# A graph network on one core: edge counts are made during both attention passes, their sort comes first, the maximum sweeps run beside the sage products

## The chip, the cores and the metric

The kernel is written in Bass for Trainium2 and runs on one core of one chip. Its engines (PE for products, DVE for vector work, ACT for activations, POOL, SP for DMA) each run their own list of instructions in order, and wait for each other by semaphores. The metric is the device time of one execution in microseconds, lower is better. Before the change the median of three runs is 3654.17 us (3653.41 to 3660.13).

## The reference, cut to what matters

3125 nodes with 128 features and 50000 edges, sorted by target. Four graph layers follow each other, each with a residual and a layer norm:

```python
x = layernorm(x + L0(x))   # edge MLP on [x[src], edge_attr], mean over each target's edges, node MLP
x = layernorm(x + L1(x))   # two attention convolutions ("gat1" 4 heads, "gat2" 1 head)
x = layernorm(x + L2(x))   # three sage convolutions: h @ Ws + (segment_sum(h[src], dst) / deg) @ Wn + b
x = layernorm(x + L3(x))   # softmax aggregation: m = x[src] + edge_attr, segment_max, exp, segment_sum
```

L2 needs, for every pair of nodes, how many edges go from one to the other; the kernel makes these counts itself and then sums neighbours by matrix products. L3's segment_max is split: the maximum of the edge features over each target's run is found by running scans over the edges, forwards and backwards, which need no node value.

## The kernel before, in words

Nodes are 26 tiles of 128 (NT). Edges are 391 blocks of 128 (NB); in the edge passes they are 416 steps (S), four to a group, 104 groups (NG).

**Order of stages.** Head: loads, tables, a sort of the edges into steps. "mlp" pass over the 104 groups (edge_products, add_node_terms, exponentials_of_hidden, join_hidden, sum_hidden, add_sums). Node work. gat1 pass, node work, gat2 pass (attention_pass on each engine). Sort of the steps of counting (place_windows on PE, sort_into_windows and place_steps on DVE). Layer norm. Counting (count_edges on PE, mark_cells on DVE, read_pairs on ACT, store_counts on SP). Sage (sum_neighbours on PE, convert on ACT and DVE, load_counts on SP). Layer norm. Pool pass. Output.

**An edge pass.** POOL gathers the rows of four steps for each group by indirect DMA (L712 for mlp, L725 for gat, L739 for pool). In mlp the ring takes 12 groups; in gat 24. The pass loops on every engine are written out by slot q. In a gat slot DVE does: the batch stages of eight groups (logits, carries, maxima; L1768 to L1817), add_sums of group q - 13 (L1561), weigh of group q - 11 (L1838, L1840, which read the turned weights in PSUM), mark_nodes of q + 1 (L1741, from a row that SP loads, L584, two buffers), and one sweep (L1759 in gat1, L1761 in gat2). PE sums the weighted rows (L955) after weigh.

**Sweeps.** 196 scans of 128 x 512 (SWEEPS = 2 x 98). SP loads 256 KB of values and 128 KB of borders for each (L599, L601) and stores 256 KB (L609), two buffers each way. Sweep v waits for the store of sweep v - 2.

**Counting.** The sorted edges are cut into 598 steps (BUILD), each at most 128 edges of one window of 16 targets (SPAN; 208 windows). A step is two products into a bank of PSUM: a product with zeros that clears it if its window is new (L1036), and low_marks x cell_marks (L1039). DVE makes these two bf16 marks of each step by is_equal (L2103, L2105). Two steps make a pair; ACT copies both banks to 16-bit counts (L1367), SP stores two rows of 100 KB (L649). Two chains run, one from each end, on two banks each, and are joined where they meet (MEET = 300).

**Sage.** The counts are loaded by chunks of 512 targets (L661, WIDTHS = six of 512 and one of 128, per layer, three layers). ACT converts the even and DVE the odd of 25 slices of a chunk to float (L1377, L2126), seven slices in hand (SLICES); PE multiplies each (L1116), in sage1 twice. The load of chunk n waits until chunk n - 2 is converted. PE makes the own part of the chunk before after slice 10 (L1053 to L1062) and its rows after slice 20 (L1084 to L1090).

## Time and profile before

| | us |
|---|---|
| median of three runs | 3654.17 |
| profiled execution, device time | 3656.58 |
| its span, first to last instruction | 3654.7 |

The page cuts the span into 40 slices of 91 us. Digits are tenths of the slice that each engine is busy; PEclk is TensorE's granted clock, DMA the share of the 16 DMA engines.

```profile
## 2 busy tenths in 40 slices
PE   6777778344444423444453777789999995666666
PEld 4665665234444323344342333335544543555554
DVE  5888885567777756787667666621111226666668
ACT  2887886334433232433322666633211234444443
POOL 4777760477777357777730000000000004777770
PEclk9999999655555555555556999989999997888886
DMA  6555550577777266777710545453321334555550
GB/s 205 154 160 155 161 143 11 140 194 201 205 198 203 51 169 176 201 196 206 198 36 14 163 162 164 161 157 92 98 72 45 108 117 112 148 148 151 150 147 26
```

POOL's line shows the four gathering passes (slices 1 to 6, 8 to 14, 15 to 21, 34 to 39). Between slices 21 and 33 POOL has nothing to do: sort and norm, counting (DMA at 5), then sage (PE at 9).

### The profile page before, as it was taken

The numbers are of one execution on the slowest core, as the hardware profiler recorded it, in microseconds if no ns is written. First come the engines' busy times: TensorE is split into PE (matmuls) and PEld (weight loads), VectorE is DVE, ScalarE is ACT, GpSimd is POOL, SyncE is SP. The second block draws the span as 40 slices with busy tenths as digits, with TensorE's granted clock in tenths as the row PEclk, the third lists the DMA queues.
The fourth block names the chain that finished last, engine by engine and source line by source line (L and its number), as shares of the span: only waits on it lengthen the run. The fifth ranks groups of instructions, "written<-read, shape, count | busy, mean of one in ns | idle before, by whom it ended". The sixth has DMA issues, their size and how long they took to land.

```text
span 3654.7 us, 44760 instructions
## 1 busy us (share of the span) xinstructions
PE 2391.6 (65%) x9865; PEld 1648.7 (45%) x9865; DVE 2257.3 (62%) x6047; ACT 1621.9 (44%) x3304; POOL 1622.4 (44%) x1620
## 2 busy tenths in 40 slices
PE   6777778344444423444453777789999995666666
PEld 4665665234444323344342333335544543555554
DVE  5888885567777756787667666621111226666668
ACT  2887886334433232433322666633211234444443
POOL 4777760477777357777730000000000004777770
PEclk9999999655555555555556999989999997888886
DMA  6555550577777266777710545453321334555550
GB/s 205 154 160 155 161 143 11 140 194 201 205 198 203 51 169 176 201 196 206 198 36 14 163 162 164 161 157 92 98 72 45 108 117 112 148 148 151 150 147 26
DMA packets 675621, 511.58 MB, mean 140 GB/s; under 512 B 66405, under 2 KB 641758, under 8 KB 675024
## 3 DMA queue, kind: packets, MB, share of 16 engines
q1 hardware_dynamic: 614422, 370.87, 34.6%
q0 software_dynamic: 57904, 132.57, 14.5%
q10 hardware_dynamic: 3052, 5.38, 0.5%
q8 instruction: 94, 1.54, 0.2%
q14 instruction: 149, 1.22, 0.1%
HBM read 385.39 MB, written 123.19 MB: 139 GB/s over the span
## 4 chain that ended last, share of the span: by engine, by line
PE 28%; POOL 27%; DVE 16%; issue 14%; SPq 8%; DMA 3%; DVEq 2%; ACT 1%; POOLq 0%; ACTq 0%
POOL big L725 16%; PE ps L1116 15%; POOL y_and_h L739 11%; SPq L649 6%; PE ps L856 5%; DVE y_and_h L1589 3%; DVE big L1561 3%; DVE ps L1581 2%; PE ps L792 1%; SPq L644 1%; DMA big<-table_gat,big 1%; PE ps L778 1%; DVEq L494 1%; PE ps L955 1%; DVE w_sb L1759 1%
## 5 line engine op out<-in xcount | busy, mean ns | idle before, releaser
L725 POOL DMA_INDIRECT big<-table_gat,big x832 | 854.3, 1027 | 480.8 <-issue 247.8
L739 POOL DMA_INDIRECT y_and_h<-table_pool,src_block x391 | 396.5, 1014 | 1309.6 <-DMA table_pool<-x_sb 1190.7
L1561 DVE TENSOR_TENSOR big<-big,ps 128x257 f32 (+3 forms) x1664 | 590.8, 355 | 226.3 <-issue 22.4
L955 PE MATMUL ps<-y_and_h,work 128*128 128x136 f32 (+1 forms) x1664 | 437.0, 443 | 413.1 <-DVE y_and_h L1840 393.1
L955 PEld LDWEIGHTS ps<-y_and_h,work 128*128 128x128 f32 x1664 | 373.6, 325 | 443.1 <-DVE y_and_h L1840 442.9
L712 POOL DMA_INDIRECT big<-table_mlp,src_block x391 | 370.9, 948 | 158.8 <-issue 117.6
L1304 ACT ACTIVATE work<-iota,dst_rel 128x128 f32<-128x128 f32 x936 | 296.0, 387 | 68.8 <-PE ps L955 68.8
L1326 ACT ACTIVATE y_and_h<-y_and_h 128x128 f32<-128x128 f32 (+1 forms) x26 | 8.0, 309 | 670.9 <-DVE y_and_h L1817 670.9
L1367 ACT ACTIVATE work<-ps 128x800 uint16<-128x800 f32 x298 | 244.5, 836 | 136.3 <-DMA adjacency<-work 84.3
L856 PE MATMUL ps<-w_sb,work 128*128 128x256 f32 x832 | 210.9, 398 | 127.7 <-DVE y_and_h L1589 116.9
L1147 PE MATMUL ps<-big,y_and_h 128*128 x624 | 203.1, 483 | 129.5 <-DVE big L2210 128.3
L1036 PE MATMUL ps<-work 128*128 128x400 bf16 x598 | 211.3, 353 | 100.7 <-ACT work L1367 91.3
L856 PEld LDWEIGHTS ps<-w_sb,work 128*128 128x128 f32 x832 | 152.4, 193 | 185.7 <-DVE y_and_h L1589 158.0
L2103 DVE TENSOR_SCALAR work<-work,big 128x128 bf16<-128x128 bf16 x598 | 149.1, 249 | 135.9 <-PE ps L1039 135.8
L1147 PEld LDWEIGHTS ps<-big,y_and_h 128*128 128x128 f32 x624 | 141.9, 238 | 167.5 <-issue 144.6
L1039 PE MATMUL ps<-work 128*128 128x400 bf16 x598 | 213.9, 358 | 0.2
L865 PE MATMUL ps<-y_and_h,work 128*128 128x257 f32 x832 | 198.8, 381 | 3.5 <-DVE big L1561 3.5
L1116 PE MATMUL ps<-w_sb,big 128*128 128x512 f32 (+1 forms) x500 | 196.2, 545 | 0.7 <-DVE w_sb L2126 0.7
L2105 DVE TENSOR_SCALAR work<-work,big 128x400 bf16<-128x400 bf16 x598 | 189.9, 318 | 0.0
L1432 ACT ACTIVATE big<-ps 128x512 f32<-128x512 f32 x98 | 58.4, 596 | 282.4 <-DVE ps L2204 282.4
L1308 ACT ACTIVATE work<-work,ones 128x512 f32<-128x512 f32 x234 | 168.9, 722 | 7.6
L920 PE MATMUL ps<-big 128*128 x832 | 76.6, 183 | 145.9 <-DVE big L1741 82.2
(349 smaller groups left out, 4394.9 us busy)
## 6 DMA issues: line engine op xcount, KB each, us to landing
adjacency<-work SPq DMA_DIRECT2D x598, 100.0 KB, 1.7
work<-adjacency SPq DMA_DIRECT2D x9, 3200.0 KB, 11.9
big<-adjacency SPq DMA_DIRECT2D x9, 3200.0 KB, 11.9
work<-in_ea_blocks SPq DMA_DIRECT2D x416, 64.0 KB
work<-rel_rows SPq DMA_DIRECT2D x208, 128.0 KB
w_sb<-in_ea_blocks SPq DMA_DIRECT2D x97, 256.0 KB, 3.0
w_sb<-border_dram SPq DMA_DIRECT2D x194, 128.0 KB, 3.9
prefix_blocks<-w_sb SPq DMA_DIRECT2D x97, 256.0 KB
```

The costliest lines, as they stand in the source:

```text
L649: sp.dma_start(adjacency[bass.ds(places[2 * c + odd], 1), :, :].rearrange("o p e -> p (o e)"), staged[:, n % STAGED, odd, :]).then_inc(sta ...
L712: pool.indirect_dma_start(ring[:, (block + RING_FIRST[k]) % (n * G), :], None, table[k], bass.IndirectOffsetOnAxis(src_block[:, block:bloc ...
L725: pool.indirect_dma_start(ring[:, step % GAT_RING, :], None, table[k], bass.IndirectOffsetOnAxis(src_idx[:, step:step + 1], 0))\
L739: pool.indirect_dma_start(pool_rows[q][:, i, :], None, table["pool"], bass.IndirectOffsetOnAxis(src_block[:, block:block + 1], 0)).then_in ...
L856: mm = pe.matmul(pre(g % 2)[:, j, :], ea_sb[:, g % 2, j, :], weight("W1a", 1), start=True, stop=True)
L955: mm = pe.matmul(sums_bank(g, j, width), onehot_of(k, g)[:, j, :], weighted[:, g % 2, j, 0:width], start=True, stop=True)
L1039: mm = pe.matmul(cells(banks[4 + 2 * c + half_of]), low_marks[:, slot, :], cell_marks[:, slot, :], start=False, stop=False, skip_group_che ...
L1116: mm = pe.matmul(ps[:, bank, 0:WIDTHS[c]], left, counts, start=(hi == 0), stop=(hi == HIGH - 1))
L1147: mm = pe.matmul(sums_bank(g, j, 2 * D), onehot_of("pool", g)[:, j, :], weighted_edges[:, bass.ds(slots_of[j], 1), :].rearrange("p o f -> ...
L1304: ins = act.activation(onehot_of(k, g)[:, j, :], iota[:, 0:P], ACT.Square, bias=dst_rel[:, g * G + j:g * G + j + 1], scale=-1.0)
L1367: act.activation(staged[:, n % STAGED, :, :], ps[:, 2 * c:2 * c + 2, 0:CELLS], ACT.Copy)\
L1561: dve.tensor_tensor(to, to, bank_of(j), ALU.add).then_inc(accumulated, 1)
```

## The change

What it does, stage by stage:

- The sort of counting moves to the head. ints_to_floats, split_sources and find_below run on DVE before the table additions; sort_into_windows runs before the mlp loop, with find_slots("pool") ahead of it. POOL's first gathers and PE's first products wait for KEYS_KEPT, ACT's zeroing for EDGES_MOVED. Keys are kept as bf16 in `work`; place_steps runs before the gat1 pass.
- Counting has one chain instead of two, on PSUM banks 6 and 7, with parity choosing the bank. Its 299 pairs are spread over the 416 half slots of both gat passes (pairs_at): DVE marks those of slot q at the end of its slot q, PE and ACT handle them in their slot q + 1, SP stores them in its group q + 3, between the loads of target rows.
- PSUM is freed for it: the turned weights of gat go to bank 1, ACT copies them to SBUF (copy_weights) and weigh reads that copy; the sums use banks 2 to 5.
- Sweeps leave the gat passes and run in sage, spread by its columns (sweeps_after); four load buffers instead of two, two store buffers as before.
- Chunks have 384 targets (eight, and one of 128). Chunk 0 is loaded at the end of gat2, chunk 1 after the norm, chunk n + 2 when chunk n is converted.

The diff, cut to its core:

```diff
-WIDTHS = [512] * 6 + [128]
+WIDTHS = [384] * 8 + [128]
...
+HALF_SLOTS = 2 * len(GAT) * NG
+def pairs_at(n, q, part):
+    u = 2 * (n * NG + q) + part
+    return [p for p in range(PAIRS) if p * HALF_SLOTS // PAIRS == u] if 0 <= q < NG else []
...
+SWEEP_WORK = [WIDTHS[c] * (2 if k == "sage1" else 1) for k in LAYERS for c in range(NCHUNK)]
+def sweeps_after(n, part, parts):
+    done = sum(SWEEP_WORK[:n]) * parts + SWEEP_WORK[n] * part
+    ends = [SWEEPS * at // (sum(SWEEP_WORK) * parts) for at in (done, done + SWEEP_WORK[n])]
+    return range(*ends)
...
-                j, b = sweep_group(n), n % 2
-                if n >= 2:
-                    sp.wait_ge(swept, n)
+                j, b = sweep_group(n), n % 4
+                if n >= 4:
+                    sp.wait_ge(swept, n - 2)
                 sp.dma_start(sweep_in[b][:, 0:size_of(j), :], blocks_of(ea_blocks if n < NBG else prefix_blocks, j))\
...
+            def move_sweeps(n):
+                if n == 0:
+                    sp.wait_ge(borders_stored, 32)
+                    sp.wait_ge(swept, 1)
+                if n == NBG:
+                    for last in range(NBG - 2, NBG):
+                        store_sweep(last)
+                    for b in range(2):
+                        sp.wait_ge(sweep_stored[b], 16 * (NBG // 2))
+                if n in (0, NBG):
+                    load_sweep(n)
+                    load_sweep(n + 1)
+                if n + 2 < (NBG if n < NBG else SWEEPS):
+                    load_sweep(n + 2)
+                if n % NBG >= 2:
+                    store_sweep(n - 2)
...
+            def store_pairs(pairs):
+                if pairs and pairs[0] == 0:
+                    sp.wait_ge(windows_by_dve, BUILD_READY)
+                for p in pairs:
+                    places = nc.values_load_multi_w_load_instructions(
+                        place_i[0:1, 2 * p:2 * p + 2], engines=(mybir.EngineType.SP,), min_val=0, max_val=NW + BUILD - 1,
+                        skip_runtime_bounds_check_because="the merge path, counted on the chip, stays in the grid")[1]
+                    sp.wait_ge(pair_read, p + 1)
+                    for odd in range(2):
+                        sp.dma_start(adjacency[bass.ds(places[odd], 1), :, :].rearrange("o p e -> p (o e)"),
+                                     staged[:, p % STAGED, odd, :]).then_inc(staged_out[p % STAGED], 16)
...
-                    if g < NBG:
-                        load_sweep(n * NBG + g)
-                    if 2 <= g < NBG + 2:
-                        store_sweep(n * NBG + g - 2)
...
+                    store_pairs(pairs_at(n, g - 3, 0) + pairs_at(n, g - 3, 1))
+                for g in range(NG, NG + 3):
+                    store_pairs(pairs_at(n, g - 3, 0) + pairs_at(n, g - 3, 1))
...
+                def load_chunk(n):
+                    c, nw = n % NCHUNK, WIDTHS[n % NCHUNK] // SPAN
                     sp.dma_start(counts_in[n % 2][:, 0:nw, :], adjacency[STARTS[c] // SPAN:STARTS[c] // SPAN + nw, :, :]
                                  .rearrange("w p e -> p w e")).then_inc(counts_loaded[n % 2], 16)
+                for q in range(STAGED):
+                    sp.wait_ge(staged_out[q], 32 * len(range(q, PAIRS, STAGED)))
+                sp.wait_ge(accumulated, sums_before("gat2") + G * NG)
+                load_chunk(0)
+                sp.wait_ge(x_ready, 2 * NPACK)
+                load_chunk(1)
+                for k, c, n in chunks():
+                    for part in range(HIGH // 2):
+                        for v in sweeps_after(n, part, HIGH // 2):
+                            move_sweeps(v)
+                    if n + 2 < 3 * NCHUNK:
+                        for by in range(2):
+                            sp.wait_ge(slice_ready[by], converted(n + 1, by))
+                        load_chunk(n + 2)
+                for last in range(SWEEPS - 2, SWEEPS):
+                    store_sweep(last)
...
             pool.wait_ge(src_loaded, 16)
+            pool.wait_ge(windows_by_dve, KEYS_KEPT)
             gather_blocks("mlp", pre_ready, 0, LAG)
             gather_steps("gat1")
...
             pe.wait_ge(read_by["dve"], fills_read(FIRST_FILL["flag"], "dve"))
+            place_windows()
+            pe.wait_ge(windows_by_dve, KEYS_KEPT)
             for g in range(NG + 2):
...
+            def count_pairs(pairs):
+                if pairs and pairs[0] == 0:
+                    pe.wait_ge(windows_by_dve, BUILD_READY)
+                for p in pairs:
+                    banks = nc.values_load_multi_w_load_instructions(
+                        bank_i[0:1, 4 * p:4 * p + 4], engines=(mybir.EngineType.PE,), min_val=BUILD_BANK, max_val=BUILD_BANK + 1,
+                        skip_runtime_bounds_check_because="a bank is found from a parity")[1]
+                    if p:
+                        pe.wait_ge(pair_read, p)
+                    for i in range(2):
+                        step = 2 * p + i
+                        pe.wait_ge(cells_marked, step + 1)
+                        pe.wait_ge(lows_marked, step + 1)
+                        pe.matmul(cells(banks[i]), nothing, cell_no, start=True, stop=False, skip_group_check=True)
+                        mm = pe.matmul(cells(banks[2 + i]), low_marks[:, step % KEYS, :], cell_marks[step % KEYS],
+                                       start=False, stop=False, skip_group_check=True)
+                    mm.then_inc(pair_built, 1)
...
                     if x:
                         pe.wait_ge(below_max_ready, batch_at + x)
+                        pe.wait_ge(weights_copied, batch_at + x)
+                        pe.wait_ge(weighed, at + (x - 1) * BATCH + 2)
...
+                        mm = pe.transpose(ps[:, 1, P + i * R:P + (i + 1) * R], weights_T[0:R, i, :], ident[0:R, 0:R])
...
+                    count_pairs(pairs_at(n, q - 1, 0))
                     if q >= WEIGH:
                         sum_weighted(q - WEIGH)
...
+                    count_pairs(pairs_at(n, q - 1, 1))
...
+            act.wait_ge(windows_by_pe, EDGES_MOVED)
...
+                def copy_weights(x):
+                    act.wait_ge(weights_turned, batch_at + x + 1)
+                    if x >= 2:
+                        act.wait_ge(weighed, n * NG + (x - 1) * BATCH)
+                    act.activation(weight_cols[:, x % 2, 0:2 * R], ps[:, 1, P:P + 2 * R], ACT.Copy).then_inc(weights_copied, 1)
+                def read_pairs(pairs):
+                    for p in pairs:
+                        act.wait_ge(pair_built, p + 1)
+                        if p >= STAGED:
+                            act.wait_ge(staged_out[p % STAGED], staged_before(p))
+                        act.activation(staged[:, p % STAGED, :, :], ps[:, BUILD_BANK:BUILD_BANK + 2, 0:CELLS], ACT.Copy)\
+                           .then_inc(pair_read, 1)
                 for q in range(NG + WEIGH):
                     x, s = divmod(q - BATCH - 2, BATCH)
                     if s == 0 and 0 <= x < NK:
                         make_weights(x)
                         if x:
                             scale_carry(x)
+                        copy_weights(x)
+                    read_pairs(pairs_at(n, q - 1, 0))
                     if MARK <= q < NG + MARK:
                         mark_nodes_of(k, q - MARK)
+                    read_pairs(pairs_at(n, q - 1, 1))
...
+            ints_to_floats()
+            split_sources()
+            find_below()
...
+            find_slots("mlp")
+            find_slots("pool")
+            sort_into_windows()
             link(dve.memset(elus[:, :, :, 256:257], 1.0))
-            find_slots("mlp")
...
+            def mark_pairs(pairs):
+                for p in pairs:
+                    if p >= KEYS // 2:
+                        dve.wait_ge(pair_built, p - KEYS // 2 + 1)
+                    for step in (2 * p, 2 * p + 1):
+                        dve.tensor_scalar(low_marks[:, step % KEYS, :], low_no, low_key[:, step:step + 1], None, ALU.is_equal)\
+                           .then_inc(lows_marked, 1)
+                        dve.tensor_scalar(cell_marks[step % KEYS], cell_no, cell_key[:, step:step + 1], None, ALU.is_equal)\
+                           .then_inc(cells_marked, 1)
...
-                        dve.wait_ge(weights_turned, batch_at + x + 1)
+                        dve.wait_ge(weights_copied, batch_at + x + 1)
                     steps = slice(s * G, (s + 1) * G)
                     slot_at = g * G % GAT_RING
-                    both = ps[:, 2 + x % 2, 0:2 * R]
+                    both = weight_cols[:, x % 2, 0:2 * R]
...
-                    if k == "gat2" and q in SORTING:
-                        SORTING[q]()
...
-                    if q < NBG:
-                        sweep(n * NBG + q)
+                    mark_pairs(pairs_at(n, q, 0) + pairs_at(n, q, 1))
...
+            place_steps()
...
-            find_slots("pool")
-            sort_into_windows()
-            place_steps()
             norm(2, *attention_output("gat2", sums_of_gat2))
...
+            def sweep(n):
+                b, j = n % 2, sweep_group(n)
+                dve.wait_ge(sweep_loaded[n % 4], 32 * (n // 4 + 1))
+                if n >= 2:
+                    dve.wait_ge(sweep_stored[b], 16 * (n // 2))
+                dve.wait_ge(swept, n + 1)
+                to, values = words(sweep_out[b], j), words(sweep_in[n % 4], j)
+                borders = sweep_borders[n % 4][:, 0:size_of(j) * P]
+                before = sweep_out[1 - b].rearrange("p g e -> p (g e)")
+                if n < NBG:
+                    ins = dve.tensor_tensor_scan(to, borders, values, before[:, G * P - 1:G * P], ALU.add, ALU.max)
+                else:
+                    ins = dve.tensor_tensor_scan(to[:, ::-1], borders[:, ::-1], values[:, ::-1], before[:, 0:1], ALU.add, ALU.max)
+                ins.then_inc(swept, 1)
...
+                    for v in sweeps_after(n, hi // 2, HIGH // 2):
+                        sweep(v)
```

## Rows read from the trace of the kernel before

**Rows 1.** Busy time by windows: start:end, length, each engine's us and instructions, clock, DMA.
```profile
800.00:1200.00 400.00, 187.63 (x934) 165.71 (x934) 302.30 (x813) 142.51 (x378) 307.49 (x304) 0.50 0.75 200
1315.00:1345.00 30.00, 4.16 (x28) 2.93 (x28) 11.41 (x17) 0.00 (x0) 23.33 (x22) 0.50 0.85 225
2001.00:2379.00 378.00, 277.26 (x1186) 116.61 (x1187) 246.85 (x1180) 243.67 (x298) 0.00 (x0) 0.95 0.50 162
2397.00:2576.00 179.00, 178.57 (x494) 91.06 (x494) 35.59 (x91) 65.97 (x111) 0.00 (x0) 0.99 0.39 119
2576.00:2890.00 314.00, 312.93 (x951) 157.70 (x952) 52.89 (x115) 61.80 (x108) 0.00 (x0) 1.00 0.22 67
2890.00:3033.00 143.00, 140.66 (x394) 66.96 (x393) 38.19 (x114) 54.23 (x98) 0.00 (x0) 1.00 0.36 110
```

**Rows 2.** Timeline (start, us, engine, line, operation, count, idle before): PE around the counting.
```profile
1998.41 0.84 PE L1021 MATMUL ps<-work 128*128 128x400 bf16 x4 [0.60 <-ACT big L1208]
...
2397.13 1.22 PE L1116 MATMUL ps<-work,x_sb 128*128 128x512 f32 x1 [17.61 <-ACT work L1377]
```

**Rows 3.** Timeline of the sort: first count, last of the keys, first after it.
```profile
1903.84 0.47 PE L975 MATMUL ps<-ones,big 98*104 98x1 f32 x2 [1.88 <-DVE big L1561]
...
1941.61 0.47 DVE L1943 TENSOR_SCALAR big<-big 128x598 f32<-128x598 f32 x1
...
1957.33 0.20 DVE L2005 TENSOR_TENSOR big<-y_and_h 128x26 f32<-128x26 f32 x1
```

**Rows 4.** Timeline of the first edge pass: gathers (L712) first and last, slots, group 97, end.
```profile
36.32 1.10 POOL L712 DMA_INDIRECT big<-table_mlp,src_block  x1 [34.94 <-DMA table_mlp<-big]
...
55.92 0.57 DVE L1479 CAST work<-big 1x416 f32<-1x416 int32 x1
...
530.11 0.95 POOL L712 DMA_INDIRECT big<-table_mlp,src_block  x1 [0.30 <-issue]
...
541.09 1.10 DVE L1581 TENSOR_TENSOR ps<-ps,big 128x256 f32<-128x256 f32 x3 [0.19 <-issue]
...
581.67 0.18 DVE L1625 TENSOR_SCALAR stat<-big 128x26 f32<-128x26 f32 x1
```

**Rows 5.** By line: gathers in 100 to 500 and 1400 to 1800 us, min/median/max ns.
```profile
L712 POOL DMA_INDIRECT big<-table_mlp,src_block x318: 942/946/1073, 102.5 to 498.8; - x159
...
L725 POOL DMA_INDIRECT big<-table_gat,big x299: 940/944/1934, 1399.3 to 1798.9; - x150
```

**Rows 6.** Groups by line, 1540 to 1560 us: part of the sort's first half.
```profile
L1889 DVE TENSOR_TENSOR xT<-xT 98x512 f32<-98x512 f32 x5 | 3.6, 714 | 0.2
```

**Rows 7.** Waits of DVE, 740 to 1190 us: us in total, times, longest.
```profile
DVE big L1741 <- DMA work<-rel_rows: 37.6, 13, 3.5
DVE y_and_h L1773 <- DMA big<-table_gat,big: 19.9, 8, 7.1
```

**Rows 8.** Groups by line, 740 to 1190 us: busy us, mean ns, idle before.
```profile
L1759 DVE TENSOR_TENSOR_SCAN w_sb<-w_sb 128x512 f32<-128x512 bf16 x84 | 107.2, 1276 | 0.7 <-DVE chain L1746 0.4
```

**Rows 9.** Timeline of DVE in the counting: one step's mark and the next's.
```profile
2103.06 0.25 DVE L2103 TENSOR_SCALAR work<-work,big 128x128 bf16<-128x128 bf16 x1 [3.27 <-PE ps L1039]
...
2103.46 0.25 DVE L2103 TENSOR_SCALAR work<-work,big 128x128 bf16<-128x128 bf16 x1
```

**Rows 10.** The page: ACT's read of a pair; DMA issues, us to landing last.
```profile
L1367 ACT ACTIVATE work<-ps 128x800 uint16<-128x800 f32 x298 | 244.5, 836 | 136.3 <-DMA adjacency<-work 84.3
...
adjacency<-work SPq DMA_DIRECT2D x598, 100.0 KB, 1.7
work<-adjacency SPq DMA_DIRECT2D x9, 3200.0 KB, 11.9
```

**Rows 11.** Timeline: a load issued behind a store, and DVE's start on what it brought.
```profile
1324.51 0.50 SPq L584 DMA_DIRECT2D work<-rel_rows  x1
...
1330.05 0.35 DVE L1741 TENSOR_SCALAR big<-work,part 128x512 bf16<-128x512 bf16 x1 [4.29 <-DMA work<-rel_rows]
```

**Rows 12.** Timeline of SP: the second load of counts, right behind the first.
```profile
2384.88 6.62 SPq L661 DMA_DIRECT2D big<-adjacency  x1
```

461 lines of the change are left out of this document (178 added, 283 removed).

## The prediction

> **What bounds the kernel now.** I read the page's 40 slices first, to cut the span into stages, then the busy time by windows, then for each stage the waits and the timeline. There are six stretches that matter. The first edge pass (to about 582 us) runs at POOL's pace: its gathers start 1.25 us apart and hardly vary [rows 4, 5]. The two attention passes are POOL's too, though less cleanly: in 400 us only 304 gathers run, one per 1.316 us, and some last up to 1934 ns instead of 944 [rows 1, 5]. PE is half idle there at a granted clock of 0.50, ACT is at 36%, DVE at 76%. Then comes a serial sort [rows 3], then the counting of edges, 399 us in which POOL does nothing and PE, DVE and ACT hand 299 pairs of steps to each other [rows 1, 2]. The sage products, 636 us in three layers of 179, 314 and 143 us, are PE's: it is busy 98 to 100% of them while DVE is at 17 to 27% and DMA at 0.22 to 0.39 [rows 1]. The change moves work from stretches where one resource waits to stretches where it is idle. So the question is what each host stretch has left.
>
> **Part 1: counting leaves its place.** From the first product of counting to the first sage product lie 2397.1 - 1998.4 = 398.7 us, with the 12 us wait for the first load of counts in it [rows 2, 12]. In the changed kernel the first chunk is loaded long before, so all but one conversion (0.6 us) and a little more goes: -397.5.
>
> **Part 2: the sort leaves its place.** PE's first count of windows starts at 1903.8 and the attention output begins at 1957.3 [rows 3]: -53.5.
>
> **Part 3: the sort comes to the head.** Its first half (the float splits, ten operations of 0.4 to 0.7 us, and some dozen copies and comparisons) adds about 10 us to DVE ahead of the 13 table additions [rows 6]. There DVE waits for PE by turns, so I let 6.5 of the 10 reach the chain. Its second half, from the first count to the finished keys with the pool slots beside it, took 1941.6 + 0.5 - 1903.8 = 38.2 us [rows 3]. About 3 us of it may go, since the page's line of slices has PE's clock at 5 to 6 tenths there and at 9 in the head (my estimate; the bounds are 0 and 6). The mlp slots began at 55.9 and take 5 us [rows 4]. The keys are then ready at 55.9 + 6.5 + 5 + 38.2 - 3 = 102.6, say 104. POOL now waits for them; before, it started at 36.3 [rows 4]. 391 gathers at 1.25 plus a landing give 492 us. From group 97, whose rows are the last that POOL brings, to the end of the pass was 581.7 - 541.1 = 40.6 us [rows 4]. So the pass ends at 104 + 492 + 41 = 637 instead of 582: +55 (45 to 62). POOL's lead of 30 us over DVE, which used to be spent over the pass, is gone; that is why the cost is more than the 42 us by which the loop starts later.
>
> **Part 4: attention passes.** What must fit is 1.44 pairs in each slot of about 5.3 us. DVE: a step's first comparison starts 0.40 us before the next step's [rows 9], so 299 steps a pass are 119 us. The 98 scans that leave are 1.28 us each, 125 us [rows 8]. So DVE's load stays, and it has spare time: over 450 us it waited 37.6 us for the target rows and 19.9 us for gathers [rows 7], 13%. ACT: 149.5 reads of 0.84 us [rows 10] are 125 us in a pass in which ACT is 36% busy. PE: counting's 1186 products took 277.3 us at a clock of 0.95, so a pair's four take 0.94 us there and up to 1.9 at half clock, which lifts its 47% by 36 to 51 points if the clock stays. It should rise instead, as it did in counting (73% busy, 0.95) [rows 1]. The single chain needs PE, ACT and a store of 1.7 us [rows 10] in a slot or two, which it has. DMA loses the sweeps' traffic and gets far less. POOL: without the scans the long gathers should be rarer, towards the 1.25 of the first pass: 416 x 0.066 = up to 27 us a pass.
>
> First what the rows say: where DVE runs scans with both operands in SBUF, gathers last up to 1934 ns; in the first pass, whose additions read PSUM, never over 1073 [rows 5]. The Trainium skill's page "SBUF — State Buffer", section "Who interferes with whom", says that VectorE takes a port pair shared with GpSimd in two-port modes of copy and tensor_scalar too, so the bf16 marks would do what the scans did. No row here shows marks beside gathers; by the page the gain of 27 us would be nothing or a loss.
>
> Against the gain stand new waits: SP now issues two stores for each pair between the target-row loads and waits for ACT's read first, and ACT stands between the turned weights and DVE. place_steps (about 13 us) sits in front of the first pass, where DVE has nothing due until the first batch of gathers: +3. For both passes together I take -15 (bounds -55 and +65, the gain of all long gathers and 0.3 us a slot for the loop through SP).
>
> **Part 5: sage.** PE's products keep their columns, and the weight loads, busy for half the time [rows 1], have room for the shorter ones, so I leave its time as it was. Cost comes from the 196 sweeps, with four rules in SP's and DVE's order. (a) Sweep v on DVE waits until the store of sweep v - 2 has landed. (b) That store is issued behind two loads, 0.95 us after the sweep ends. (c) A chunk of counts (2.4 MB) is loaded when the chunk before has been converted, and the next store is queued behind it. (d) DVE is in order, so a sweep that waits holds up the odd slices, and PE has seven slices in hand.
>
> Two sweeps thus need 0.95 + the landing + 1.2. The nearest rows: a load issued behind a store landed after 5.5 us in a stretch whose DMA share was 0.85 [rows 1, 11], and a lone 100 KB store in 1.7 [rows 10]. In sage there are no gathers; I take 3.9, so 6.0 us for two sweeps (bounds 5 and 8.3, the spacing of two in the stretch of rows 11). The chunk load: 3.2 MB took 11.9 us to land [rows 10], and a second one behind it held SP for 6.6 us [rows 12]; so one load passes in about 7 us for 2.4 MB, and a store queued behind it lands some 11.5 us after the chunk was converted. 5.9 sweeps then take a sage0 or sage2 chunk to about 25.5 us; PE needs 179 x 384/3200 = 21.5 in sage0 and 17.2 in sage2. A sage1 chunk has 11.8 sweeps, about 43.5 us against 37.7. Over 8.33 chunks each: 33 + 48 + 69 = +150. With 5 us a pair and DVE's waits hidden it is +60, with 8.3 us +250 and more.
>
> On (c), the row is that second load, which held SP until the first had nearly passed [rows 12]. The skill's page "DMA: Bandwidth & Descriptors", section "Queues, rings and completion order", says each engine consumes one row's descriptors in ring order. If instead SP's transfers overtook each other, the 11.5 would be about 5 and the loss near +60.
>
> **The sum**, against the profiled execution's span of 3654.7: - 397.5 - 53.5 + 55 + 3 - 15 + 150 = 3396.7. Around the span lie 1.9 us (3656.6 reported), and the median of the runs is 2.4 us below that: 3396. I predict 3395.
>
> **Rivals.**
> A (forecast): the sage stage becomes a chain of sweeps, stores and chunk loads; 3395, own range 3340 to 3450. Chance 0.42.
> B: the sweeps hide under the products. For it: DVE is at 17 to 27% and PE has seven slices in hand. Against it: sage2 has 2.9 us per sweep, less than any landing loop above. What is left is the spare share of DMA, +45 at most: 3395 - 105 = 3290. Chance 0.16.
> C: the passes grow. The target-row load, which already cost 37.6 us in 450 [rows 7], now waits for PE, ACT and a store; or PE at half clock is late. 0.4 us a slot over 208 slots: +83 +15, so 3490; with half of it 3445. Chance 0.22.
> D: POOL is freed of the long gathers and nothing else is late: both passes at 1.25, -40 more: 3355. Chance 0.11.
> E: the marks lock POOL out for all their time, 1.44 x 2 x 0.40 = 1.15 us a slot, on top of four gathers at 1.25: 6.15 instead of 5.3, +175 over both, so about 3580. The rule named in part 4 would give it. The page's other claim, that scans take the pair, agrees with rows 5, and those cost 4 x 0.066 = 0.27 us a slot, not 1.2. Chance 0.05.
> F, the other side: slower than before. The loop that goes weigh, sum, pair, ACT's read, store, target-row load, mark has two slots' time by the order in the code. If it has to close within one, a slot takes its whole length, 8 to 10 us: 208 x 3.7 = +770, so about 4160. It decides from 6.6 us a slot on: the forecast's 258 us, over 208 slots, are 1.25 above 5.3. For it: PE's order is strict. Against it: PE's and DVE's orders in before show the same lag of two slots, and rel_b has two buffers. Chance 0.03.
> That the kernel does not do what it says (the counting would stay on the path) I hold for excluded by the diff.
>
> **How the numbers follow.** The likeliest is A at 3395. B, D, and the milder part of C lie within 3290 to 3490; E, F and C's tail lie outside. Range 3290 to 3485. 0.2% of 3654, 7 us, is about what a measurement can tell from no change: faster 0.96, same 0.01, slower 0.03.
>
> **What would show it.** Sage's first product near 2000 - 53 + 55 - 12 = 1990. The first gather near 104 and the end of the first pass near 637. Gather spacing in the attention passes between 1.25 and 1.30. DVE's waits in sage "<- DMA" on stores or loads of sweeps, longest once a chunk at 8 to 11 us; PE under 90% busy in sage2; sage near 786 us. Wrong if sage stays under 680 us, if a slot in the passes is over 5.5 us, or if the first gather starts after 115.

## The result, and where the time went

The changed kernel takes 3510.94 us (median of four runs, 3506.3 to 3512.89) against 3654.51 before: ratio 0.960, 95% interval 0.959 to 0.962. It is faster, by 144 us where 259 were forecast, and the time lies above the range (3290 to 3485). The profiled execution has a span of 3507.8 us.

The view of 40 slices (88 us each here) of the changed kernel:

```profile
PE   6677777846656665466666478988887665666675
...
DVE  6588888557878888477777744444443346666668
...
POOL 0577776047777750777777100000000006777770
PEclk8899999966677776578777689999998887888887
DMA  4355555035555541555555277877776755555550
```

The stretch without POOL, twelve slices of 91 us before, is now ten of 88 (24 to 33), and nearly all of it is sage. DMA stands at 7 to 8 in most of it, where sage had 1 to 5 before, and TensorE's granted clock falls from 9 to 8 tenths towards its end. In the attention passes (slices 9 to 15 and 17 to 22) the clock rose from 5 tenths to 6 to 8, as forecast; only slice 17 is still at 5.

The marks between the stages come from the first gather of each pass and PE's first and last product of sage, in the timelines of POOL and PE (start, us, engine, line, operation, idle before):

```profile
110.03 1.11 POOL L751 DMA_INDIRECT big<-table_mlp,src_block  x1 [108.64 <-DVEq L1598]
...
1408.80 0.94 POOL L764 DMA_INDIRECT big<-table_gat,big  x1 [113.88 <-DMA table_gat<-y_and_h]
...
1949.42 0.94 POOL L764 DMA_INDIRECT big<-table_gat,big  x1 [0.30 <-issue]
...
2028.97 1.21 PE L1154 MATMUL ps<-work,x_sb 128*128 128x384 f32 x3 [1.02 <-ACT work L1423]
...
2884.81 0.92 PE L1154 MATMUL ps<-work,y_and_h 128*128 128x128 f32 x6
```

With gat1's first gather at 739.5 (677.6 before), gat2's at 1408.8 (1307.7 before) and sage from 2029.0 to 2885.7 (2397.1 to 3031.9 before), the balance by stages is:

| stretch | before | after | change | forecast |
|---|---|---|---|---|
| start to gat1's first gather | 677.6 | 739.5 | +61.9 | +55 |
| gat1's first gather to gat2's | 630.1 | 669.3 | +39.2 | with the next row: -12 |
| gat2's first gather to sage, sort and counting taken off | 638.4 | 620.2 | -18.2 | |
| sort and counting | 451.0 | 0 | -451.0 | -451.0 |
| sage, first to last product | 634.8 | 856.7 | +221.9 | +150 |
| from there to the end | 622.9 | 622.1 | -0.8 | 0 |

The forecast missed the span by 111 us: 7 in the head, 33 in the two attention passes, 72 in sage. The experiments go after the last two.

Sage by windows (start:end, length, each engine's us and instructions, clock, DMA share, GB/s), the three layers in turn:

```profile
2029.00:2256.00 227.00, 191.05 (x610) 116.74 (x610) 94.59 (x163) 72.26 (x143) 0.00 (x0) 0.93 0.78 228
2256.00:2645.00 389.00, 336.61 (x1169) 205.05 (x1168) 173.14 (x248) 67.85 (x139) 0.00 (x0) 0.94 0.76 219
2645.00:2885.00 240.00, 163.76 (x485) 93.10 (x486) 96.27 (x185) 59.13 (x124) 0.00 (x0) 0.84 0.70 201
```

Before, PE was busy 98 to 100% of the layers at a clock of 0.99 to 1.00 [rows 1]. Now it is at 84, 87 and 68%, and the clock is 0.84 in sage2. DVE's waits in sage2 (engine, line, who ended the wait: us in total, times, longest):

```profile
DVE big L2132 <- DMA maximum_blocks<-big: 71.5, 7, 12.4
DVE big L2132 <- issue: 35.6, 14, 5.4
DVE y_and_h L2171 <- PE ps L1107: 25.0, 8, 5.0
```

L2132 is the sweep: once in each of seven chunks it waits some 10 us for the store of the sweep before the last. SP's and DVE's timelines at one of these:

```profile
2758.63 0.37 SPq L684 DMA_DIRECT2D big<-adjacency  x1
2759.05 4.46 SPq L616 DMA_DIRECT2D w_sb<-prefix_blocks  x1
2763.55 1.16 SPq L618 DMA_DIRECT2D w_sb<-border_dram  x1
2764.75 0.44 SPq L626 DMA_DIRECT2D maximum_blocks<-big  x1
...
2770.43 1.28 DVE L2132 TENSOR_TENSOR_SCAN big<-big,w_sb 128x512 f32<-128x512 bf16 x1 [11.61 <-DMA maximum_blocks<-big]
```

The chunk (L684) is issued at 2758.6, the load behind it holds SP for 4.5 us, the store (L626) goes out 6.1 us after the chunk, and the sweep that needs it starts 11.8 us after the chunk. That is the forecast's rule (c), with its 11.5 us. Behind the other whole chunks of sage, in all three layers and with the first load beside the sweeps left aside, the trace has the same stretch at 10.3 to 13.4 us, most often 11.5 to 11.8.

### The profile page after: what moved, and what is told of

Same layout as the page of the kernel before. It is cut to its first block, busy times and chain, and to the rows that moved or that the text cites. A ratio compares the mean times of both kernels' runs of the same rounds, so it can differ in the third digit from the quotient of the medians.

```text
span 3507.8 us, 46264 instructions
## 1 busy us (share of the span) xinstructions
PE 2401.2 (68%) x10293; PEld 1677.8 (48%) x10293; DVE 2312.7 (66%) x6113; ACT 1637.0 (47%) x3421; POOL 1611.7 (46%) x1620
## 3 DMA queue, kind: packets, MB, share of 16 engines
q14 instruction: 154, 1.26, 0.1%
## 4 chain that ended last, share of the span: by engine, by line
POOL 29%; DVE 21%; issue 16%; PE 16%; DMA 9%; SPq 5%; ACT 2%; DVEq 2%; POOLq 0%; ACTq 0%
POOL y_and_h L778 11%; POOL big L764 10%; POOL big L751 7%; PE ps L1154 7%; DVE big L1715 4%; DMA maximum_blocks<-big 3%; DMA prefix_blocks<-big 3%; SPq L616 2%; PE ps L896 2%; DVE y_and_h L1989 2%; DVE big L1888 1%; SPq L671 1%; DMA work<-rel_rows 1%; SPq L618 1%; DVE big L2132 1%
## 5 line engine op out<-in xcount | busy, mean ns | idle before, releaser
L1047 PE MATMUL ps<-y_and_h,work 128*128 128x136 f32 (+1 forms) x1664 | 338.7, 365 | 213.4 <-DVE y_and_h L1991 210.5
L1379 ACT ACTIVATE w_sb<-ps 128x800 uint16<-128x800 f32 x299 | 248.7, 832 | 479.0 <-PE ps L993 478.6
L1047 PEld LDWEIGHTS ps<-y_and_h,work 128*128 128x128 f32 x1664 | 293.6, 259 | 275.1 <-DVE y_and_h L1991 272.0
L992 PE MATMUL ps<-xT 128*128 128x400 bf16 x598 | 256.4, 429 | 84.1 <-ACT w_sb L1379 65.4
L1154 PE MATMUL ps<-work,big 128*128 128x384 f32 (+1 forms) x772 | 258.8, 487 | 45.5 <-DVE work L2141 45.1
L1154 PEld LDWEIGHTS ps<-work,big 128*128 128x128 f32 x772 | 145.8, 200 | 149.1 <-DVE work L2141 57.7
L993 PE MATMUL ps<-big,w_sb 128*128 128x400 bf16 x450 | 195.5, 434 | 0.0
L1423 ACT ACTIVATE work<-work 128x384 f32<-128x384 uint16 (+1 forms) x156 | 75.8, 492 | 235.1 <-PE ps L1154 234.3
L1154 PE MATMUL ps<-work,y_and_h 128*128 128x384 f32 (+1 forms) x386 | 143.8, 517 | 58.6 <-DVE work L2141 58.0
L1989 DVE TENSOR_TENSOR y_and_h<-big,work 128x512 f32<-128x512 f32 x208 | 179.4, 862 | 1.6 <-ACT work L1371 1.4
```

Of the source, the lines that this page charges most:

```text
L992: pe.matmul(cells(banks[i]), nothing, cell_no, start=True, stop=False, skip_group_check=True)
L1047: mm = pe.matmul(sums_bank(2, g, j, width), onehot_of(k, g)[:, j, :], weighted[:, g % 2, j, 0:width], start=True, stop=True)
L1154: mm = pe.matmul(ps[:, bank, 0:WIDTHS[c]], left, counts, start=(hi == 0), stop=(hi == HIGH - 1))
L1379: act.activation(staged[:, p % STAGED, :, :], ps[:, BUILD_BANK:BUILD_BANK + 2, 0:CELLS], ACT.Copy)\
L1989: dve.tensor_tensor(weighted[:, g % 2, :, 0:D].rearrange("p g (f h) -> p g f h", h=heads), ring[:, slot_at:slot_at + G, 0:D].rearrange("p ...
```

## The experiments

All but two start from the changed kernel; e9 starts from e1, and e12 from e7. Each group was timed beside runs of the kernel before on the same chip; medians of before were 3660 in the group of e1 to e4, 3658 in that of e5 to e8, 3657 in that of e9 and e10 and 3654 in that of e11 and e12. e7 and e8 carry the edits of e1, e2 and e3. Differences of a stage are taken from the profiled executions, between the same marks as in the table. How well a stage repeats is seen in the runs whose edit leaves it alone: gat1 669 to 676 us, the gathers of gat2 1.290 to 1.303 us apart, sage 857 to 862 and sage2 238 to 242.

### e1: the heads of the copied weights side by side

```diff
-act.activation(weight_cols[:, x % 2, 0:2 * R], ps[:, 1, P:P + 2 * R], ACT.Copy)
+act.activation(weight_cols[:, x % 2, 0:2 * R].rearrange("p (k s h) -> p k h s", k=2, h=heads),
+               ps[:, 1, P:P + 2 * R].rearrange("p (k h s) -> p k h s", k=2, h=heads), ACT.Copy)
...
-p = head_rows(both[:, 0:R])[:, steps, :].unsqueeze(2)
+p = both[:, 0:R].rearrange("p (s h) -> p s h", h=heads)[:, steps, :].unsqueeze(2)
```

> ACT's copy of the turned weights is written with the heads of a step side by side instead of 32 words apart; nothing else differs from the changed kernel. Theory (gat1 grew because weigh, 0.68 us when it read PSUM, takes 1.04 when it reads the SBUF copy at that stride, and DVE is late there): weigh is back near 0.70, 104 x 0.34 = 35 us go from gat1 (its first gather to gat2's: 669 -> 634), gat2 unchanged, time 3511 -> about 3476. Rival 1 (it is SBUF in place of PSUM, whatever the stride): weigh stays over 1.0 and the time within 5 us of 3511. Rival 2 (gat1 grew because target rows queue behind the pair stores): weigh gets shorter, DVE's wait for the target rows takes the room, time over 3500.

Measured: 3487.1 us (3480 to 3497), ratio 0.953 (0.950 to 0.956) where the changed kernel has 0.960. The groups by line of DVE's weigh in gat1 show it (busy us, mean ns, idle before). Before, the changed kernel, e1:

```profile
L1838 DVE TENSOR_TENSOR y_and_h<-big,ps 128x512 f32<-128x512 f32 x83 | 56.4, 679 | 0.1
```

```profile
L1989 DVE TENSOR_TENSOR y_and_h<-big,work 128x512 f32<-128x512 f32 x78 | 81.1, 1039 | 1.6 <-ACT work L1371 1.4
```

```profile
L1991 DVE TENSOR_TENSOR y_and_h<-big,work 128x512 f32<-128x512 f32 x83 | 57.4, 692 | 2.0 <-ACT work L1371 1.8
```

Weigh had 679 ns from PSUM, 1039 from the SBUF copy with the four heads 32 words apart, and 692 with them side by side. So it is the stride and not SBUF as such: rival 1 falls. gat1 goes from 669.3 to 642.5 us, 27 less. (The edit lays out the small copy behind weigh in the same way; it takes 0.18 to 0.19 us in both.) The theory's 35 was somewhat too much, and a part of rival 2 is in it: DVE's waits for target rows in the pass rose from 69 to 81 us. The gathers' spacing in gat1 fell from 1.336 to 1.282 us as well. The Trainium skill's page "SBUF — State Buffer" (the note on cachelines in section "Door 1: The DMA port swizzle") says that SBUF reads lines of 16 bytes and that each access crossing to a new line costs; by that rule, the traces agree: 4 bytes used of each line cost 0.35 us on 512 elements, four words in one line nothing.

### e2: the store ahead of the loads

```diff
-                if n + 2 < (NBG if n < NBG else SWEEPS):
-                    load_sweep(n + 2)
                 if n % NBG >= 2:
                     store_sweep(n - 2)
+                if n + 2 < (NBG if n < NBG else SWEEPS):
+                    load_sweep(n + 2)
```

> In sage SP issues the store of sweep v - 2 ahead of the two loads of sweep v + 2 instead of behind them. Theory (a chain of sweeps and store landings outside the chunk loads, each pair of sweeps with 0.95 us of issue in it, beside a stall of 11.5 us a chunk that this doesn't touch): 98 pairs less 25 x 2 that lie in stalls, about 50 x 0.95 plus the loads' packets no longer ahead of the store: -40 to -80 us of sage's 857. Rival (the chain only decides inside the chunk-load stall, elsewhere the products' own pace does): at most -15 us.

Measured: 3433.5 us (3432 to 3436), ratio 0.938 (0.936 to 0.940). Sage falls from 856.7 to 779.3, 77 less, at the upper end of the theory's range. It is layer by layer 227 -> 210, 389 -> 356 and 240 -> 213. The long waits are still there, one a chunk, the longest 10.5 instead of 12.4:

```profile
DVE big L2132 <- DMA maximum_blocks<-big: 58.9, 7, 10.5
```

They give 12.6 of sage2's 27 us, so the edit shortens the stall as well; the rest comes from outside it. In sage1 the median from a sweep's start to that of the sweep after the next falls from 6.6 to 5.55. So outside the chunk loads too the sweeps are a chain through their stores, as the forecast had it; the rival falls.

### e3: the chunk in eight pieces

```diff
+                        if n and n + 1 < 3 * NCHUNK and part < PIECES:
+                            load_piece(n + 1, part)
...
-                    if n + 2 < 3 * NCHUNK:
-                        for by in range(2):
-                            sp.wait_ge(slice_ready[by], converted(n + 1, by))
-                        load_chunk(n + 2)
```

> A chunk of counts is loaded in eight pieces of 300 KB, one after each step of the sweeps of the chunk before, instead of 2.4 MB at once. Theory (a store queued behind the whole chunk makes DVE, and with it PE, stop 10 to 12 us a chunk): the long waits of DVE and PE go, at most 3 to 4 us are left of each, 25 x about 6 = 150 us less in sage (857 -> 700), time about 3360. Rival (the DMA engines' share, 0.78 in sage0, is what binds, and the stall only shows where its bytes fall): less than 50 us, the same time spread over more and shorter waits.

Measured: 3392.5 us (3387 to 3401), ratio 0.928 (0.925 to 0.930); sage 737.5, 119 less, where the theory said about 150 and the rival less than 50. The windows of sage2 and its longest waits:

```profile
2567.00:2762.00 195.00, 157.15 (x490) 87.70 (x489) 97.27 (x185) 59.17 (x124) 0.00 (x0) 0.95 0.86 250
```

```profile
DVE big L2140 <- issue: 53.9, 34, 2.8
...
PE ps L1162 <- DVE work L2149: 30.6, 26, 4.1
DVE big L2140 <- DMA maximum_blocks<-big: 27.9, 6, 6.5
```

The stops of PE in this layer shrink to 4.1 us at most, and its clock is back at 0.95. The stall behind the whole chunk is thus the largest single term of sage's growth. What stays, 104 us over the kernel without sweeps (e4), comes in many short waits, 34 of 1.6 us on average in sage2, and six longer ones for stores, up to 6.5 us, at a DMA share of 0.86 to 0.89: some of the rival is there too.

### e4: no sweeps

```diff
-                    for v in sweeps_after(n, hi // 2, HIGH // 2):
-                        sweep(v)
...
-                        for v in sweeps_after(n, part, HIGH // 2):
-                            move_sweeps(v)
```

> Leaves out the sweeps of the edge features' maxima with their loads and stores; the pool pass reads the edge features in place of the maxima. Theory (all of sage's growth of 222 us is the sweeps; 384 targets a chunk cost nothing): PE 98% busy, sage 857 -> 636 to 645, time about 3295. Rival (more chunk boundaries, 25 instead of 19, and shorter products cost too): sage over 660. The rest of the kernel, passes included, unchanged to 5 us.

Measured: 3288.2 us (3284 to 3292), ratio 0.898 (0.896 to 0.900). Sage takes 633.4 us, a microsecond less than before the change:

```profile
2032.00:2209.00 177.00, 176.50 (x611) 112.34 (x611) 39.17 (x116) 72.36 (x144) 0.00 (x0) 1.00 0.37 110
2209.00:2523.00 314.00, 313.65 (x1168) 199.02 (x1168) 56.51 (x149) 67.20 (x137) 0.00 (x0) 1.00 0.22 67
2523.00:2665.00 142.00, 140.83 (x489) 85.45 (x490) 41.06 (x136) 59.12 (x124) 0.00 (x0) 1.00 0.39 118
```

Chunks of 384 cost nothing; the whole +222 is the sweeps. PE is busy 631 us here and 691 in the changed kernel (the sums of the windows shown for each), for the same products. The trace has the changed kernel's TensorE at the lower level for 154 us of sage, 94 of them busy, and not at all in this run; at half the rate 94 us are 47 too many. So some 47 of the 60 us are the clock, which no term of the forecast held; the rest comes with PE's many restarts and wasn't told apart.

### e5: the chunks from POOL's queue

```diff
+            for n in range(3 * NCHUNK):
...
+                if n >= 2:
+                    for by in range(2):
+                        pool.wait_ge(slice_ready[by], converted(n - 1, by))
...
+                pool.dma_start(counts_in[n % 2][:, 0:nw, :], adjacency[STARTS[c] // SPAN:STARTS[c] // SPAN + nw, :, :]
+                               .rearrange("w p e -> p w e")).then_inc(counts_loaded[n % 2], 16)
```

> All chunks of counts are loaded whole, 2.4 MB at once, but from POOL's queue, which has nothing to do in sage, instead of SP's. Theory (the stall is the order of SP's queue: the store stands behind the chunk's descriptors): the 10 to 12 us waits of DVE are gone as with eight pieces, sage 857 -> about 740, time about 3395. Rival (it is the engines' bytes: chunk and store share the 16 DMA engines, whichever queue they come from): waits of 5 to 8 us a chunk are left, sage 780 to 820.

Measured: 3464.2 us (3458 to 3479), ratio 0.948 (0.945 to 0.951); sage 809.7, inside the rival's 780 to 820. DVE's wait for the sweep in sage2:

```profile
DVE big L2129 <- issue: 73.3, 24, 8.1
```

The longest is 8.1 us instead of 12.4, where the theory had the long waits gone. At that one the store went out at 2672.9, 4.9 us after the chunk's issue, and the sweep that needs it began at 2682.1. So SP's order is only a part of the stall: a store issued beside 2.4 MB from another queue still lands late. The Trainium skill's page "DMA: Bandwidth & Descriptors" (section "Queues, rings and completion order") has a rule for it: a semaphore's increment lands only after every earlier write of the same DMA engine, across its queues. This would give what e5 shows, though no run here tells it from plain sharing of the engines. Sage0 and sage2 gained 17 and 29 us, sage1 only 1.6 (387.5); why sage1 gained so little is open.

### e6: narrow marks

```diff
+                    lo_w, hi_w = (P, CELLS) if p < KEYS // 2 else (8, 8)
...
-                        dve.tensor_scalar(low_marks[:, step % KEYS, :], low_no, low_key[:, step:step + 1], None, ALU.is_equal)\
+                        dve.tensor_scalar(low_marks[:, step % KEYS, 0:lo_w], low_no[:, 0:lo_w], low_key[:, step:step + 1], None, ALU.is_equal)\
```

> From the fifth pair on DVE writes only 8 columns of each mark, so that the edge counts aren't made; every wait and every other instruction stays. Theory (marks cost DVE their time, and POOL's gathers little): two marks of a step 0.40 -> about 0.2 us, some 60 us less of DVE in each pass; gat1, which is DVE's, falls from 669 to about 640, gat2, which is POOL's, by at most 8 us, gather spacing there from 1.303 to no less than 1.285. Rival (the marks take the port from POOL, which is why gat2 is not at 1.25): the spacing in gat2 falls to 1.26 or less, 17 us or more.

Measured: 3481.3 us (3479 to 3490), ratio 0.952 (0.950 to 0.954). gat1 646.6 (-23), gat2's first gather to sage 607.9 (-12), its gathers 1.272 us apart instead of 1.303. The marks themselves, in gat2:

```profile
L1887 DVE TENSOR_SCALAR w_sb<-xT 128x8 bf16<-128x8 bf16 x250 | 60.8, 254 | 0.4
...
L1889 DVE TENSOR_SCALAR big<-xT 128x8 bf16<-128x8 bf16 x187 | 43.7, 260 | 0.0
```

Eight columns take 0.25 us, as 128 did [rows 9], and only the mark of 400 columns got shorter (0.36 to 0.26). So the run took away 0.1 us a step and not 0.2, and its outcome is between the two expectations: 1.272 is under the theory's 1.285 and over the rival's 1.26. Since runs with full marks have 1.290 to 1.303, it shows that the wide marks cost POOL's pass some 7 to 13 us, and it doesn't show whether the rest, down to 1.25, is the narrow ones. In gat1 the gathers got no closer (1.345); its 23 us are DVE's. The forecast's rival E, 6.15 us a slot, is refuted by the changed kernel itself: a slot of gat2 took 4 x 1.303 = 5.2 us.

### e7: e1, e2 and e3 together

> The packed weights, the store ahead of the loads, and the chunk in eight pieces, together. If each acts at its own place: -27 (gat1 as measured) and in sage more than the -119 of the pieces alone, since the pairs outside the chunk loads get shorter too: 700 to 710 us, time about 3330. If the DMA engines' bytes bind by now (share 0.86 to 0.89 with the pieces alone), the store's place gives nothing more: sage 735, time about 3360.

Measured: 3335.4 us (3327 to 3348), ratio 0.912 (0.909 to 0.914), the fastest whole kernel here: 5% under the changed one. Sage takes 709.8 us, -28 against the pieces alone, and gat1 644.6: each acts at its own place. Windows near the layers (the second cut lies 15 us inside sage2, the third ends at 2710):

```profile
2000.00:2200.00 200.00, 184.25 (x621) 112.59 (x620) 93.94 (x166) 74.49 (x148) 0.00 (x0) 0.99 0.92 263
2200.00:2540.00 340.00, 331.68 (x1219) 205.51 (x1218) 180.90 (x263) 73.29 (x148) 0.00 (x0) 1.00 0.93 263
2540.00:2710.00 170.00, 140.49 (x433) 78.56 (x432) 87.54 (x168) 52.83 (x111) 0.00 (x0) 0.94 0.90 259
```

The DMA share is 0.90 to 0.93. e8 and e12 ask whether that is the bound now.

### e8: more sweeps in sage1

```diff
-SWEEP_WORK = [WIDTHS[c] * (2 if k == "sage1" else 1) for k in LAYERS for c in range(NCHUNK)]
+SWEEP_WORK = [WIDTHS[c] * {'sage0': 10, 'sage1': 24, 'sage2': 7}[k] for k in LAYERS for c in range(NCHUNK)]
```

> As the three together, with the 196 sweeps shared out 48 : 115 : 33 over the three layers instead of 49 : 98 : 49. With the pieces the layers stood 23, 28 and 53 us over the kernel without sweeps. If a layer is late by its sweeps per us of product, sage2 loses about 35 of its 53 and sage1 gains at most 15: 15 to 25 us less than the three together. If the bytes of all sage bind evenly: within 5 us of them.

Measured: 3341.7 us (3336 to 3345), ratio 0.913 (0.912 to 0.915): as e7. Sage 716.3 against 709.8: sage2 fell from 187 to 164 us, and sage1 rose from 325 to 359. In these two splits the sweeps take their time with them.

### e9: place_steps twice

```diff
-            place_steps()
+            place_steps(False)
+            place_steps(True)
```

(the argument says whether the waiting engines are released at its end)

> With the packed weights, place_steps runs twice in a row and releases its waiters after the second time. In the packed kernel gat1 (its first gather to gat2's) stood at 642.5 us against 630.1 before, and DVE begins its slots 14 us later against the gathers. Theory (place_steps lies on the path at its full length, since DVE is the late one in gat1): gat1 642.5 -> 655 to 657. Rival (the 3 us of the forecast, DVE has nothing due and catches up): gat1 under 647.

Measured: gat1 655.9 us against 642.5 in e1, +13.4; 3494.5 us (3488 to 3497), ratio 0.955 (0.953 to 0.958) against 0.953. In DVE's timeline of the changed kernel place_steps runs from here to here:

```profile
736.83 0.37 DVE L1604 TENSOR_SCALAR xT<-iota 128x400 bf16<-128x400 f32 x1
...
750.46 0.46 DVE L1633 TENSOR_TENSOR xT<-w_sb,y_and_h 1x299 int32<-1x299 f32 x1
```

These are 14.1 us, and nearly all of them are on the path. POOL's first gather was at 739.5, so DVE begins the pass after POOL, and it never catches up: between 800 and 1250 it does not wait for a gather once, where it waited for eight of them before [rows 7].

### e10 and e11: PE kept busy through the stalls of sage2

```diff
+                        if k == "sage2" and (c, hi) in ((2, 3), (3, 3), (4, 3), (5, 5), (6, 5)):
+                            for _ in range(14):
+                                pe.matmul(ps[:, 5, 0:384], ident[:, :], inv_cols[:, 0:384], start=True, stop=True)
                         pe.wait_ge(slice_ready[hi % 2], converted(n, hi % 2) + hi // 2 + 1)
```

(27 in e10)

> The changed kernel with 27 spare products of 128 x 384 in sage2, in each of five chunks (third to seventh) ahead of the slice at which PE stood idle for 8 to 10 us; at full clock they take 27 x 0.325 = 8.8 us. Theory (PE comes out of each stall at the lower clock, and this lengthens the chunk): granted clock in sage2 from 0.84 to over 0.93, chunks shorter by 2 to 4 us each, sage2 240 -> 222 to 230 in spite of the added work. Rival (the chain of sweeps and stores sets the chunk, and PE has time to catch up): the products get faster, sage2 stays within 4 us of 240. If the spare products reach past the stall, sage2 gets longer.

e10 measured: 3535.1 us (3533 to 3544), ratio 0.968 (0.965 to 0.970); sage2 265.8 us. The spare products filled 17.6 us and reached past the stall, which the expectation had as its last case. Its clock in sage2 was 0.96.

> As the run before with 14 spare products in place of 27: a product of floats takes two passes, 0.65 us, so that 27 filled 17.6 us, twice the stall; 14 take 9.1. Theory (the lower clock after each stall lengthens the chunk): sage2, 240 us in the changed kernel, 222 to 232. Rival (the chain of sweeps and stores sets the chunk): the products at full clock, sage2 236 to 244.

e11 measured: 3499.6 us (3489 to 3506), ratio 0.957 (0.955 to 0.960) where the changed kernel has 0.960 (0.959 to 0.962); sage2 230.9 us instead of 240.2, within the theory's 222 to 232 and outside the rival's 236 to 244. PE's timeline after a stall in the changed kernel, and after the same stall with the spare products:

```profile
2711.68 1.65 PE L1154 MATMUL ps<-big,y_and_h 128*128 128x384 f32 x2 [9.89 <-DVE big L2141]
2713.12 6.33 PE L1154 MATMUL ps<-work,y_and_h 128*128 128x384 f32 x12
```

```profile
2701.97 9.19 PE L1152 MATMUL ps<-big,ident 128*128 128x384 f32 x28
2712.15 0.91 PE L1157 MATMUL ps<-big,y_and_h 128*128 128x384 f32 x2 [0.98 <-DVE big L2144]
2712.90 4.03 PE L1157 MATMUL ps<-work,y_and_h 128*128 128x384 f32 x12
```

A product of floats stands as two records (x2). Twelve records take 4.03 us at the full level (2.4 GHz). After 10 us of idleness the first two take 1.65 instead of 0.81, which is the lower level (1.2 GHz), and the next twelve 6.33. The five chunks took 150.8 us without the spare products and 142.0 with them: 1.8 us a chunk. So the lower clock after a stall is on the path in sage2: products of no use make the layer quicker. The whole time says it less sharply, since the two ratios' intervals just touch; sage2's 230.9 lies well below the 238 to 242 of the four runs that leave sage alone. The clock is not all of it: the same chunks are 30.2 us long on average, 4.7 over the 25.5 of the forecast.

### e12: e7 with few loads of borders

```diff
+                if n >= 4:
+                    return
                 sp.dma_start(sweep_borders[b][:, 0:size_of(j) * P],
```

> The three together, and the borders (128 of the 640 KB of a sweep) are loaded for the first four sweeps alone, so that the maxima aren't the reference's. Theory (with the three, sage is at the bytes: DMA share 0.92 and 710 us): a fifth of the sweeps' bytes less, sage 710 -> 660 to 680. Rival (what is left over the 633 us without sweeps is the sweeps' own chain of landings, about 4 us from a store's issue): within 10 us of 710.

Measured: 3283.9 us (3278 to 3287), ratio 0.898 (0.897 to 0.900); sage 663.9, 46 less than e7, within the theory's 660 to 680.

```profile
1998.00:2180.00 182.00, 177.77 (x609) 111.41 (x610) 92.76 (x163) 72.42 (x144) 0.00 (x0) 1.00 0.87 251
2180.00:2500.00 320.00, 317.57 (x1179) 199.60 (x1178) 174.76 (x253) 69.19 (x140) 0.00 (x0) 1.00 0.79 229
2500.00:2655.00 155.00, 138.54 (x439) 78.55 (x438) 89.55 (x166) 55.31 (x113) 0.00 (x0) 0.99 0.90 267
```

A fifth of the sweeps' bytes is gone, with the same scans, stores and waits, and with it 46 of the 76 us that e7 stands over the kernel without sweeps. So the larger part of what is left in e7 hangs on the loads of the borders. That it is their bytes which bind is likely, with the DMA share down from 0.93 to 0.79 in sage1, but not shown: the run also takes one of SP's three issues of a sweep away, 0.5 to 1.2 us, and how much of the 46 that is wasn't told apart.

## Why the prediction was wrong

The likeliest case had the right mechanism in sage and the right places in the passes, with several terms too small, in every part but the first two. It was rival A with 111 us on top, of which part is the direction of rival C, though not by its mechanism.

**Parts 1 and 2, counting and sort leave (-451).** Right: between gat2's first gather and sage nothing of either is left, and conversions wait for no chunk. The first product came at 2029 instead of 1990, by the misses of the head (7) and of the passes (33). DVE's first sweep then waited 11.2 us for its loads, but from 2022.5 to 2033.7, with PE already at work.

**Part 3, the head (+55; measured +61.9).** Two steps were in error. "I let 6.5 of the 10 reach the chain": the slots begin at 64.8, 8.9 us later than before [rows 4], which is 2.4 of the miss. And "about 3 us of it may go": nothing went, PE's 48 products in the middle of the sort took 14.7 us both before and in the head. The keys are ready at 109.0 instead of 102.6. The gathers at 1.25 and the tail were right (391 gathers from 110.0 to 598.2, end at 643.9 for 637 forecast).

**Part 4, the passes (-15 and +3; measured +21).** Three terms failed. place_steps was taken at 3 us, on the ground that DVE has nothing due before the first gathers land; it costs 13.4 by e9 and its 14.1 us in the timeline. The ground was false because gat1 became DVE's: it had no wait for gathers left in which to catch up, and its waits for target rows did not take the delay up. And weigh, which reads the SBUF copy, was costed at nothing. The prediction named ACT between the turned weights and DVE as a new wait, which is 1.4 us in all, and overlooked what the copy does to the read itself: 104 x 0.36 = 37 us of DVE's time, of which e1 gave back 27.

The third term is "So DVE's load stays". Two windows of 450 us in gat1, before and after:

```profile
740.00:1190.00 450.00, 209.82 (x1046) 185.55 (x1046) 336.55 (x898) 165.25 (x438) 346.06 (x342) 0.50 0.74 200
```

```profile
800.00:1250.00 450.00, 285.56 (x1454) 193.63 (x1452) 356.31 (x1230) 253.56 (x545) 347.61 (x336) 0.72 0.52 129
```

They hold 84 slots before (the scans of rows 8) and 78 after (weigh, L1989), so a slot took 5.4 us before and 5.8 now (the prediction's own sign of being wrong was 5.5), and kept DVE busy for 4.01 us and then for 4.57. Of the 0.56 more, 0.36 is weigh; the other 0.20, some 21 us over 104 slots, is what the marks take beyond the scans (an estimate). Against this, DVE waited 32.9 us for gathers in gat1 before and not at all after. That makes 58 + 13 + 3 (target rows) - 33 = 41 for the +39.2. That 13.4 + 27 from e9 and e1 also comes near it is thus in part luck. (The 36 to 51 points forecast for PE don't follow from 0.94 to 1.9 us a pair, which are 25 to 52 points of a slot; the windows have PE at 47 and 63%.)

The gain of rarer long gathers came in gat2 as expected, 1.303 us instead of 1.343, worth 17 of its 18.2 us. In gat1 it did not: the gathers were 1.336 us apart for 1.320 before, though POOL waited only 1.8 us for DVE. In the two windows above, the gathers that overlap weigh lasted 944 ns on average when weigh read PSUM and 1178 when it read the SBUF copy. With e1's shorter weigh they are 1.282 us apart. So the copy at that stride lengthened the gathers too, which the prediction did not count. Rival C's loop through SP did not grow: DVE's waits for target rows in gat1 were 65.8 us before and 69.0 after. Rivals D, E and F fall: no pass was at 1.25, no slot at 6.15, and the kernel got faster.

**Part 5, sage (+150; measured +222).** Rules (a) to (d) hold as written. The stall behind a chunk, from its issue to the sweep that needs the next store, was 11.5 forecast and is 11.8 in the rows shown. By the layers the forecast of 33, 48 and 69 met 48, 75 and 97. The terms that were too small:
- "so I left its time as it was", of PE. After each stall PE comes back at the lower clock: its busy time rose from 631 to 691 us, some 47 of that by the clock, and e11 showed 1.8 us a chunk of it on the path in sage2. For sage0 and sage1 no run tells the clock apart. The prediction had just read in rows 1 that the clock goes with PE's idleness, and used it for the passes alone.
- The pair of sweeps at 6.0 us. In sage1, where most pairs lie outside a stall, the median from a sweep's start to that of the sweep after the next is 6.6. With (11.8 - 2) / 2 = 4.9 such pairs a chunk that is 4.9 x 0.6 x 8.33 = 24 of the 27 us by which sage1 missed (an estimate). In sage0 the median is 6.7, and 1.95 such pairs a chunk make some 11 of its 15.
- In the five whole chunks of e11's comparison sage2 missed 4.7 us a chunk, of which the clock is 1.8. The rest fits with DVE waiting for PE's turned sums in the chunk (L2171, 3.1 us a time), a wait that the chain of sweeps then inherits. This is argued, no run took that wait away.

e5 also bears on the prediction's "if instead SP's transfers overtook each other": with the chunk in another queue the longest waits of the sweeps in sage2 are still 5 to 8 us and the growth of sage is 175, far from the "near +60" that was given for transfers that overtake each other. Rival B (hidden sweeps, 3290) fell, though its time is what e4 gives without any sweep: with the order in SP's queue mended, sage still stands at 710, and 46 of the 76 us left go with the borders' loads, a fifth of the sweeps' bytes (e7, e12).

## What to carry to other kernels

When work is laid beside a stage that keeps PE full, price every stall twice: once for the wait, and once for the products after it at the lower clock. A small store whose landing is waited for belongs ahead of the loads in its queue, and a transfer of megabytes in that queue belongs in pieces: these two edits were worth 147 us of sage's 222, while another split of the sweeps over the layers gained nothing (e8). A copy that moves an operand from PSUM to SBUF should be laid out for its reader, with what is read together side by side. When an engine stops waiting for another, its own terms begin to count: in gat1 DVE's waits for gathers went, and place_steps (e9), weigh (e1) and the marks (e6) each came onto the path.

## What was not expected of the hardware

- A DVE product of 128 x 512 floats took 0.69 us with its second operand's four words side by side in SBUF or anywhere in PSUM, and 1.04 with them 32 words apart in SBUF (e1).
- A bf16 comparison of 8 columns takes 0.25 us, as long as one of 128; one of 400 took 0.36 beside the gathers (e6).
- A store issued beside a load of 2.4 MB from another engine's queue still held its waiter for up to 8.1 us (e5), against 12.4 in the same queue.
- Gathers that overlap a DVE product with both operands in SBUF at that stride lasted 1178 ns on average, and 944 when one operand came from PSUM.
- A float product of 128 x 384 fills 0.65 us of PE, in two records of 0.325, at the full clock (e10).
